# The projections of a two-layer kernel: x laid out by channels too, normalised on VectorE by rows, and zeros multiplied first

## The reference, cut to what matters

```
def _layernorm(x, axis=-1, eps=1e-05):
    m = jnp.mean(x, axis=axis, keepdims=True)
    v = jnp.var(x, axis=axis, keepdims=True)
    return (x - m) / jnp.sqrt(v + eps)
...
x1 = x @ w1_w.T + w1_b
x_conv = _silu(_depthwise_conv(x1, conv_w))
x_ssm = _ssm(x_conv, A, B_ssm, C_ssm, D_ssm)
v = _silu(x @ v1_w.T + v1_b)
return x_ssm * v @ w2_w.T + w2_b
...
xn = _layernorm(x, axis=-1)
x = x + _L0_attn_ref(xn, ...) + _L0_ffn_ref(xn, L0_ffn_weight, L0_ffn_bias)
xn = _layernorm(x, axis=-1)
x = x + _L1_attn_ref(xn, ...) + _L1_ffn_ref(xn, ...)
```

## Time and profile before

| | us |
|---|---|
| device time, median of 3 runs | 2106.39 (2106.2 to 2106.66) |
| the profiled execution's own time | 2105.94 |
| its span, first to last instruction | 2104.1 |
| TensorE busy | 2079.7 |
| VectorE busy | 1475.4 |
| ScalarE busy | 1092.0 |
| GpSimd busy | 842.2 |
| the first stage on TensorE, first transpose to the scan's first matmul | 11.63 to 394.94 |

### The profile page before, as it was taken

How to read it: one execution, slowest core, us unless ns; L and a number is a source line. 1 busy time by engine, 2 the same in 40 slices (tenths; PEclk the granted TensorE clock), 3 DMA queues, 4 the chain that set the end, 5 groups by cost and what they waited for, 6 DMA issues and landing times.

```text
span 2104.1 us, 27600 instructions
## 1 busy us (share of the span) xinstructions
PE 2079.7 (99%) x9467; PEld 1666.6 (79%) x9467; DVE 1475.4 (70%) x2884; ACT 1092.0 (52%) x1834; POOL 842.2 (40%) x844
## 2 busy tenths in 40 slices
PE   7999999999999999999999999999999999999998
PEld 6888888644578888888888888888888888888887
DVE  4776555576687777776777876576777767677776
ACT  4554555423355555555555554755545555555443
POOL 1021000254554445454455454144454444544454
PEclk9999999999999999999999999999999999999999
DMA  4333533677543333333333333522222222222211
GB/s 154 120 130 126 170 127 106 230 245 235 181 139 115 106 118 113 106 115 100 120 126 106 106 115 100 170 81 71 71 71 71 71 93 89 94 77 71 71 41 41
DMA packets 174822, 241.40 MB, mean 115 GB/s; under 512 B 19033, under 2 KB 109401, under 8 KB 173914
## 3 DMA queue, kind: packets, MB, share of 16 engines
q1 hardware_dynamic: 161560, 216.10, 31.5%
q10 hardware_dynamic: 13122, 23.53, 3.0%
HBM read 138.86 MB, written 100.73 MB: 114 GB/s over the span
## 4 chain that ended last, share of the span: by engine, by line
PE 91%; DVE 5%; ACT 2%; issue 1%; POOL 1%; DMA 0%; SPq 0%; POOLq 0%; ACTq 0%
PE bank L102 23%; PE bank L104 23%; PE bank L103 23%; PE bank L1389 7%; PE bank L1945 3%; PE bank L778 3%; PE bank L799 3%; PE bank L796 3%; PE bank L1345 2%; PE bank L496 1%; DVE e_w_lo L1772 0%; DVE d_x L1241 0%; DVE d_xq L1212 0%; DVE d_stats L1243 0%; PE bank L1403 0%
## 5 line engine op out<-in xcount | busy, mean ns | idle before, releaser
L102 PE MATMUL bank<-e_ring,e_w_hi 128*128 128x512 f32 x512 | 200.8, 392 | 0.0
L103 PE MATMUL bank<-e_ring,e_w_hi 128*128 128x512 f32 x512 | 199.3, 389 | 0.0
L104 PE MATMUL bank<-e_ring,e_w_lo 128*128 128x512 f32 x512 | 199.3, 389 | 0.0
L1389 PE MATMUL bank<-d_kh,d_nat 128*128 128x512 f32 x768 | 191.2, 398 | 0.0
L1665 POOL TENSOR_TENSOR e_x<-e_x,e_beta 128x512 f32<-128x512 f32 x64 | 91.5, 1450 | 220.6 <-ACT e_y L1708 220.6
L1010 POOL TENSOR_TENSOR rstd<-d_var_eps,neg_half 128x1 f32<-128x1 f32 x64 | 35.7, 558 | 340.3 <-DVE d_var_eps L1252 340.3
L1719 ACT ACTIVATE e_kr<-bank 128x512 f32<-128x512 f32 x64 | 38.0, 594 | 247.6 <-PE bank L104 247.6
L1389 PEld LDWEIGHTS bank<-d_kh,d_nat 128*128 128x128 f32 x768 | 139.7, 188 | 26.9
L1790 DVE TENSOR_TENSOR e_ring<-e_mixed,e_ring 128x512 fp32r<-128x512 f32 x128 | 93.5, 731 | 88.1 <-ACT e_ring L1683 88.0
L1647 POOL TENSOR_TENSOR e_x<-e_x,e_ff 128x512 f32<-128x512 f32 x64 | 83.4, 1304 | 174.8 <-DVE e_ff L1856 174.8
L1257 DVE TENSOR_TENSOR d_nat<-d_xn,d_nat 128x512 fp32r<-128x512 f32 x64 | 86.0, 1344 | 77.9 <-ACT d_nat L1117 77.9
(11 more groups left out here) (210 smaller groups left out, 6291.1 us busy)
## 6 DMA issues: line engine op xcount, KB each, us to landing
scr_v<-b_vt SPq DMA_DIRECT2D x64, 256.0 KB, 2.6
scr_z<-b_zt SPq DMA_DIRECT2D x64, 256.0 KB, 2.1
c_z<-scr_z SPq DMA_DIRECT2D x64, 256.0 KB, 4.3
scr_y<-c_y ACTq DMA_DIRECT2D x64, 256.0 KB, 3.9
d_x<-in_L_attn_x SPq DMA_DIRECT2D x64, 256.0 KB, 3.7
d_v<-scr_v SPq DMA_DIRECT2D x32, 512.0 KB, 5.1
scr_x<-d_x SPq DMA_DIRECT2D x64, 256.0 KB, 2.6
scr_xnt<-d_xt SPq DMA_DIRECT2D x32, 512.0 KB, 4.1
```

The lines of the kernel that those rows point to most:

```text
L102: eng.matmul(out, lhs[hi], rhs[hi], start=first, stop=False, skip_group_check=onto)
L103: eng.matmul(out, lhs[hi], rhs[lo], start=False, stop=False, skip_group_check=onto)
L104: return eng.matmul(out, lhs[lo], rhs[hi], start=False, stop=last, skip_group_check=onto)
L1389: mm = pe.matmul(BG[c][:, :], s[:, i, cols], r[:, j, :], start=M % NTB == 0 and i == j, stop=M % NTB == NTB - 1 and i == 1, skip_group_che ...
```

## The change

Group 0 still takes x as tokens, into `xc[0]`, and is turned on TensorE, now into four banks (`TB` is two banks and the two of `KB`). For groups 1 to 15 a second copy of x, laid out by channels on the host (`x_turned`), is loaded as one DMA of 1 MB into one of two channel buffers `xc`. Mean and rstd of a token now run along the free dimension there, so they are needed as rows on every partition: SP stores the group's two columns of statistics to DRAM (`store_rows`, one element at a time), and loads them back broadcast to 128 partitions (`load_rows`). VectorE then subtracts and multiplies with plain `tensor_tensor`, eight instructions of 128x512. Statistics still come from x by tokens, now in one buffer `xg`, and are taken three groups ahead. No transposes are left for groups 1 to 15. Each normalised block is read by ScalarE and VectorE from `xc`.

On ScalarE the high parts of the next group move from the v half into the x1 half of a group's work; on VectorE the low parts move between the side terms. The ring of x1 has 6 slots instead of 8. The power steps on GpSimd are spread over groups 4 to 13; the small matmuls come after group 6. Ahead of the first transposes TensorE multiplies zeros: 6 matmuls, then 2, 1 and 1 as the statistics of group 0 go on. The low part of w1 is shared by GpSimd and VectorE. Semaphores of the later stages are merged; their order is otherwise as it was.

```diff
-    xg = [sb(f"b_xg{h}", [P, GT, D]) for h in range(2)]
+    xg = sb("b_xg", [P, GT, D])
+    xc = [sb(f"b_xc{h}", [P, KT, GN]) for h in range(2)]
...
+        def load_channels(g):
+            if g > 1:
+                sp.wait_ge(xn_done, 2 * KT * (g - 1) + KT)
+                sp.wait_ge(lo_done, KT * (g - 1))
+            sp.dma_start(xc[g % 2][:, :, :], ins["x_turned"][g]).then_inc(xc_in, 16)
+        def store_rows(g):
+            sp.wait_ge(stat, 4 * g + 4)
+            for w, name in enumerate(("mean0", "rstd0")):
+                sp.dma_start(scr["rows"][g, w].rearrange("a i -> i a"), keep[name][:, g * GT:(g + 1) * GT],
+                             allow_slow_non_contiguous=True).then_inc(rows_out, 16)
+        def load_rows(g):
+            sp.wait_ge(rows_out, 32 * g)
+            if g > 1:
+                sp.wait_ge(xn_done, 2 * KT * (g - 1) + KT)
+            sp.dma_start(rows[:, :, :].rearrange("p w t -> p (w t)"),
+                         scr["rows"][g].rearrange("w a i -> (w a i)").rearrange("(o t) -> o t", o=1)
+                         .broadcast_to([P, 2 * GN])).then_inc(rows_in, 16)
...
         for g in range(NG):
             if g + 2 < NG:
-                sp.wait_ge(t_full, KT * (g + 1))
-                load_x(g + 2)
+                load_rows(g + 2)
+                load_channels(g + 2)
+            if g + 4 < NG:
+                sp.wait_ge(stat, 4 * (g + 3) + 1)
+                load_x(g + 4)
+            if g + 3 < NG:
+                store_rows(g + 3)
...
+        def normalise(g):
+            dve.wait_ge(xc_in, 16 * g)
+            dve.wait_ge(rows_in, 16 * g)
+            for kt in range(KT):
+                nc.vector.tensor_tensor(channels(g, kt), channels(g, kt), row(0), ALU.subtract).then_inc(xn_done, 1)
+            for kt in range(KT):
+                dve.wait_ge(xn_done, 2 * KT * g - KT + kt + 1)
+                nc.vector.tensor_tensor(channels(g, kt), channels(g, kt), row(1), ALU.mult).then_inc(xn_done, 1)
...
         def body(g):
+            if g == 0:
+                weight_low(v1, v1_raw)
+                statistics(2)
             if g + 1 < NG:
                 normalise(g + 1)
-            if g == 0:
-                weight_low(v1, v1_raw)
+            if g + 3 < NG:
+                statistics(g + 3)
             for kt in range(KT):
                 for c in units_in(g):
                     side_terms(c, kt)
+                if g + 1 < NG and kt < 2:
+                    low_part(g + 1, 2 * kt)
+                    low_part(g + 1, 2 * kt + 1)
...
+        nc.vector.memset(vt[0][:, 0, :], 0.0).then_inc(warm, 1)
+        statistics(0)
+        normalise_first()
+        for kt in (2, 3):
+            dve.wait_ge(w_hi, kt + 1)
+            nc.vector.tensor_tensor(w1[:, 1, kt, :], w1_raw[:, kt, :], w1[:, 0, kt, :].bitcast(F32),
+                                    ALU.subtract).then_inc(w1_lo[1], 1)
         for kt in range(KT):
             low_part(0, kt)
+        statistics(1)
...
                 if m:
                     for c in units_in(g):
                         middle(c, m - 1)
+                if g + 1 < NG and m in (1, 2):
+                    high_part(g + 1, 2 * m - 2)
+                    high_part(g + 1, 2 * m - 1)
...
-                if g + 1 < NG and m in (0, 2):
-                    turn_x(g + 1, m)
-                    turn_x(g + 1, m + 1)
-            if g == 5:
+            if g == 6:
...
+        pe.wait_ge(warm, 1)
+        multiply_zeros(6)
+        pe.wait_ge(stat, 1)
+        multiply_zeros(2)
+        pe.wait_ge(rstd_done, 1)
+        multiply_zeros(1)
+        pe.wait_ge(xn_done, 2)
+        multiply_zeros(1)
         pe.wait_ge(const_in, 32)
         for kt in range(KT):
-            turn_x(0, kt)
+            turn_first(kt)
```

More of the change, by code:

```diff
@@ L134, in phase_project @@
     kpad = sb("b_kpad", [OCTET, NO, 2 * CHUNK])
-    const_in, tab_in = sem("b_const_in"), sem("b_tab_in")
-    x_in = [sem(f"b_x_in{h}") for h in range(2)]
+    rows = sb("b_rows", [P, 2, GN])
+    const_in, tab_in = sem("b_const_in"), keep["tables_in"]
+    x_in, xc_in = sem("b_x_in"), sem("b_xc_in")
+    rows_out, rows_in = sem("b_rows_out"), sem("b_rows_in")
     x_head = keep["x_ld"]
     w_in = [sem(f"b_w_in{i}") for i in range(2)]
-    w_hi, w_lo, w1_lo = keep["w_hi"], keep["w_lo"], sem("b_w1_lo")
+    w_hi, w_lo, w1_lo = keep["w_hi"], keep["w_lo"], [sem(f"b_w1_lo{i}") for i in range(2)]
+    warm = sem("b_warm")
     stat = sem("b_stat")
@@ L167, in phase_project, with x_stat, channels, row @@
     }
+    def x_stat(g):
+        return xg if g else xc[0]
+    def channels(g, kt):
+        return xc[g % 2][:, kt, :]
+    def row(w):
+        return rows[:, w, :]
+    def normalised(g, kt):
+        return xc[g % 2][:, kt, :] if g else TB[kt][:, :]
     def x1_row(b, r, kt):
@@ L274, in gpsimd, with statistics @@
         pool.wait_ge(keep["set"], 1)
-        for g in range(NG):
-            rstd_of(g)
-            if g == 0:
[L278 to L285, removed]
+        rstd_of(0)
+        pool.wait_ge(xn_done, GT)
+        for kt in range(2):
+            pool.wait_ge(w_hi, kt + 1)
+            nc.gpsimd.tensor_tensor(w1[:, 1, kt, :], w1_raw[:, kt, :], w1[:, 0, kt, :].bitcast(F32),
+                                    ALU.subtract).then_inc(w1_lo[0], 1)
+        rstd_of(1)
+        rstd_of(2)
+        for g in range(NG):
+            if g + 3 < NG:
+                rstd_of(g + 3)
+            if 4 <= g < 14:
+                power_step(g - 4)
     def vector(dve):
-        def normalise(g):
-            h = g % 2
+        def statistics(g):
             if g:
-                dve.wait_ge(x_in[h], 32 * ((g - 1) // 2 + 1))
+                dve.wait_ge(x_in, 32 * g)
             for t in range(GT):
@@ L409, in high_part @@
         def high_part(g, kt):
[L410 to L411 removed]
+            if g:
+                act.wait_ge(xn_done, 2 * KT * g + kt + 1)
+            else:
+                act.wait_ge(t_full, kt + 1)
+            nc.scalar.activation(xt[g % 2][:, 0, kt, :], normalised(g, kt), ACT.Copy).then_inc(hi_done, 1)
         def weight_high(i, tile, raw):
@@ L530, in body, with multiply_zeros @@
                       .then_inc(k_full, 1)
+        def multiply_zeros(n):
+            for i in range(n):
+                pe.matmul(VB[i % 2][:, :], vt[0][:, 0, 0:P], vt[0][:, 0, :], start=True, stop=True)
+        pe.wait_ge(warm, 1)
[6 more added lines that the diff above has]
+        multiply_zeros(1)
         pe.wait_ge(const_in, 32)
         for kt in range(KT):
-            turn_x(0, kt)
+            turn_first(kt)
         for g in range(NG):
@@ L621, in gpsimd @@
     def gpsimd(pool):
-        pool.wait_ge(*project["turned"])
+        pool.wait_ge(*project["split"])
         pool.wait_ge(*project["powers"])
-        pool.wait_ge(keep["toep_in"], 16 * OCTET)
+        pool.wait_ge(keep["tables_in"], 64 + 16 * OCTET)
         blocks = mask8.unsqueeze(2).broadcast_to([P, OCTET, CHUNK])
```

126 lines of the change are left out of this document (64 added, 62 removed).

## The result

The changed kernel takes 2091.98 us (median of 4 runs, 2091.68 to 2093.48) against 2106.52 us before (2106.2 to 2106.82): ratio 0.9933, 95% interval 0.992 to 0.9945. That is 14.5 us faster. The forecast was 2085.5 in a range of 2080 to 2094: the sign and the stated range held, the gain forecast, 20.9 us, was 1.4 times what came.

The account below looks back on a forecast made before the run. TensorE, busy 2079.7 of 2104.1 us, was taken as the bound. 2105.94 - 24.4 for transposes + 3.7 for a longer start = 2085.2, set at 2085.5 us after adjusting to the median; range 2080 to 2094.

Parts of the forecast that it names:

- What it removes: First stage, TensorE: the transpose blocks in groups 1 to 14 go, 14 x 2 x 0.87 = 24.4 us.
- What hides the rest: First stage: added work of VectorE (about 18 of 21.84 us a group), ScalarE and DMA is hidden, costing nothing.
- Rivals 3 and 4: First stage: 3, VectorE becomes the bound, 2125 us, chance 0.05; 4, ScalarE waits for channels each group, 2103 to 2108, 0.03.
- the signs that were named: Period 21.84 us; group 0 stand 5 to 9 us; slow pitch after; VectorE idle 2 to 4 us; rows within 5.
- DMA share: First stage, each group: (9.0 + 4.5 + 0.9) / 21.84 = 0.66 of the DMA engines' time.
- The stand: v part of group 0: TensorE stands from 30.0 to 37.2, its bank's silu being behind ScalarE's high parts of group 1.
- I take 3 us for a store: Start: landing of the single-element stores of group 1's statistics, taken as 3 us, bounds 2.0 and 10.9.
- The clock: Behind the stand in group 0: 4.1 us at half speed, 2.0 lost, bounded by 0 and 3.3 lost.
- rival 2: Start: slow single-element stores, time 2092 to 2100 us, chance 0.07.
- rivals 1 and 2: Rival 1: no stall in group 0, time 2079.2 us, chance 0.04; rival 2 has its own line.
- The zeros: Start: multiplications by zeros keep TensorE at work; what zeros, banks and shorter start win ends in a longer stand at 30.0.

Follow-up runs that it names:

- the run with the filled stand: The changed kernel with 52 matmuls into an unused bank before the third block of v of group 0, keeping TensorE working: 2091.14 us, ratio 0.9928.
- the run with both cures: The changed kernel with statistics turned on VectorE, stored in 128-byte pieces, and late high and low parts in groups 0 and 1: 2080.59 us, ratio 0.9873.

## Why the prediction was right, and where its size was off

**What it removes: right.** 24.4 us forecast for the blocks of transposes; the periods shrank by 14 x 1.82 = 25.5, a little more, as the 96 matmuls ran at 0.2267 us instead of 0.2275.

**What hides the rest: right.** The eight tensor_tensors went at four in 2.50 and 2.49 us, as the splitting of v1 had suggested. After the start TensorE has no wait in a group. Rivals 3 and 4 did not come. Of the signs that were named, one failed: the loads of rows landed within 5 us for group 1 (4.32), but took 5.6 in the median.

**DMA share: wrong, and harmless in the steady part.** Forecast 0.66, measured 0.82 in the mean of the eight windows. The forecast's 4.5 us a group for the added bytes was good: with 16-byte pieces the same queue has 66 us more than before over the span (35.0% of 2082.7 less 31.5% of 2104.1), 4.4 us a group. One term was not: "so 1024 pieces 0.9 us". The 1024 pieces of 4 bytes cost 4.2 us more than 256 pieces of 16 bytes do, and with 4.2 the forecast's sum gives 0.81. I had priced them by the 64-byte pieces of another load, which are larger, and read from DRAM and not written to it; which of the two makes the difference, no run here tells.

**The stand: the mechanism right, its length too short.** It is where the prediction put it, after 31 us in the v part of group 0, behind ScalarE's high parts. From the start of normalising to the silu that frees the bank the prediction has 28.6 to 37.2, 8.6 us; the chain has 34.31 to 42.9, 8.6 us. What failed is the term ahead of it: "I take 3 us for a store". It took 9.59 us. The loads of rows took 4.32 against 4.8. The statistics of group 2 ended at 30.9 against 27.5 forecast, as their x landed later, but did not gate. So normalising was 5.7 us late.

**The clock: right in kind, 1 us short.** 2.0 us taken within 0 to 3.3, from 4.1 us at half speed; the slow pitch lasted 6.1 us, and the run with the filled stand gives 2.85.

The two misses are 5.7 + 0.9 = 6.6 us, and group 1 begins 6.65 us after the 44.7 of the prediction. What came is therefore rival 2, slow single-element stores, on the edge of its 2092 to 2100, to which I gave 0.07. The forecast as worked out, with its own range of 2081.5 to 2091.5 and a chance of 0.81, just missed; the stated range held because parts of rivals 1 and 2 had been taken into it. The row of 64-byte pieces (4.6 us) spoke against it and I let it decide. The Trainium skill's rule on a non-contiguous last dimension (DMA: Bandwidth & Descriptors, Rules for kernel authors) spoke for it, and the trace agrees: the page of the profile counts 16320 packets under 512 B more than before, and 15 groups x 1024 pieces are 15360 of them.

```profile
DMA packets 194981, 265.04 MB, mean 127 GB/s; under 512 B 35353, under 2 KB 125721, under 8 KB 192154
```

(19033 before.) The Trainium skill's rule in TensorE: Matmul & The Clock Gate, Part 1, that an idle array falls back to 1.2 GHz, is borne out by the granted clock of 0.50 from 36 to 44 us.

**The zeros: right in the result, by less than was thought.** They bring nothing that can be told from noise in the changed kernel, and 2 us in the one before. That their win "ends in a longer stand" is not shown: without them the stand did not shrink, and the first block of v began no later than in other executions with them. There was next to no win to lose, since the matmuls had the fast pitch from 15.25 us on without them.

## What to carry to other kernels

When work moves to a side path, look for the one place where nothing hides it, which is usually the first group, and follow the in-order queue of the engine that serves two readers: here ScalarE stood for data of the next group in front of the outputs of this one. Price a transfer by the number and size of its pieces, not by its bytes alone; columns that are wanted as rows are turned on an engine first (a 32x32-block transpose took 0.21 us here) and stored in long pieces. Change an order only in the group that needs it: the same cure applied to the next group too cost about 3 us (2080.59 against 2077.69).

## What the runs showed of the hardware

Stores of 4-byte pieces are dear twice. They occupy the DMA engines (4.2 us of all 16 for 1024 pieces, beyond what the same bytes take in 256 pieces, as above), and they land late: in the changed kernel the second store of group 1 was issued at 20.29 and landed at 29.88, though the engines were quiet from 24 us on.

```profile
22.00:24.00 2.00, 2.00 (x11) 1.65 (x10) 0.24 (x1) 0.00 (x0) 0.00 (x0) 1.00 0.45 43
24.00:26.00 2.00, 2.00 (x11) 1.65 (x10) 0.00 (x0) 0.00 (x0) 0.00 (x0) 1.00 0.00 0
26.00:28.00 2.00, 2.00 (x11) 1.65 (x10) 1.45 (x3) 0.00 (x0) 0.00 (x0) 1.00 0.00 0
28.00:30.00 2.00, 2.00 (x10) 1.67 (x9) 1.64 (x9) 0.00 (x0) 0.28 (x1) 1.00 0.00 0
```

The load of x of group 2, issued before these stores, was also waited for until 26.55, though its bytes had moved by 24; with the rows turned it was there at 23.97 in the run with both cures. What the completions waited for in those 6 us, no run here tells.
